# Second chunk's rows split between GpSimd and VectorE, and a reordered last finish, in a transformer layer kernel

## The reference, cut to what matters

```python
x = x + attn(layernorm(x), w_qkv, w_out)      # 16 heads of 8, rotary embedding, causal
h = layernorm(x)
logits = h @ router_W.T + router_b            # 6 experts
gate = softmax(logits); keep the 2 largest
w = kept / (sum(kept) + 1e-6)
low = (h @ routed_A[e].T) for each e          # rank 16
x = x + h @ base_W.T + base_b                 # base
      + (h @ shared_A.T) @ shared_B.T         # shared, rank 16
      + sum_e w[e] * (low[e] @ routed_B[e].T) # routed
```

## Time and profile before

| | us |
|---|---|
| median of 3 runs | 298.48 |
| lowest, highest | 298.29, 298.51 |
| profiled execution, device time | 298.24 |
| its span in the trace | 296.5 |

### The profile page before, as it was taken

How to read it: one execution, slowest core, us unless ns; L and a number is a source line. 1 busy time by engine, 2 the same in 40 slices (tenths; PEclk the granted TensorE clock), 3 DMA queues, 4 the chain that set the end, 5 groups by cost and what they waited for, 6 DMA issues and landing times.

```text
span 296.5 us, 7512 instructions
## 1 busy us (share of the span) xinstructions
PE 279.1 (94%) x3002; PEld 102.4 (35%) x3002; DVE 139.6 (47%) x420; ACT 267.3 (90%) x303; POOL 65.4 (22%) x145
## 2 busy tenths in 40 slices
PE   7869989899999999999999999999999999999996
PEld 2624332222132222122233124445433435445343
DVE  6876866687141558526171036522113262541054
ACT  8647899899999999999998999999999998999910
POOL 3576455514304012040030121010101010103000
PEclk9999999999999999999999999999999999999999
DMA  6443434004610000000000700001000001000000
GB/s 204 116 103 88 128 90 128 0 3 107 155 59 2 4 0 2 0 0 2 2 0 18 214 22 2 2 2 38 0 3 2 2 3 35 2 2 2 21 0 18
DMA packets 15256, 11.75 MB, mean 40 GB/s; under 512 B 2081, under 2 KB 14226, under 8 KB 15218
## 3 DMA queue, kind: packets, MB, share of 16 engines
q1 hardware_dynamic: 14594, 10.64, 13.0%
q0 software_dynamic: 192, 0.39, 0.5%
q10 hardware_dynamic: 432, 0.20, 0.3%
HBM read 3.88 MB, written 1.05 MB: 17 GB/s over the span
## 4 chain that ended last, share of the span: by engine, by line
PE 49%; ACT 25%; issue 14%; DVE 8%; DMA 2%; SPq 0%; ACTq 0%; DVEq 0%
ACT pbuf L713 24%; PE po L1147 22%; PE ps L1124 13%; PE ps L1270 2%; PE ps L1163 2%; PE pm L1163 1%; PE pm L1208 1%; PE pm L1157 1%; DMA qst<-parts 1%; PE pm L1169 1%; PE pm L1214 1%; PE pm L1222 1%; DVE rest L797 1%; DMA xs<-x_dram 1%; PE pm L1218 1%
## 5 line engine op out<-in xcount | busy, mean ns | idle before, releaser
L713 ACT ACTIVATE pbuf<-ps 128x1024 f32<-128x1024 f32 (+1 forms) x280 | 253.8, 1074 | 12.0 <-PE ps L1124 11.2
L1147 PE MATMUL po<-pbuf,va 128*9 128x256 f32 (+3 forms) x1792 | 143.8, 426 | 1.5 <-DVE oq L777 1.0
L1124 PE MATMUL ps<-qst,kst 64*128 64x256 bf16 (+3 forms) x896 | 97.6, 297 | 7.6 <-ACT pbuf L713 3.1
L649 POOL TENSOR_SCALAR_AFFINE_SELECT pbuf<-pbuf 128x256 f32<-128x256 f32 (+1 forms) x104 | 47.7, 481 | 196.4 <-ACT pbuf L713 195.2
L1124 PEld LDWEIGHTS ps<-qst,kst 64*128 64x128 bf16 x896 | 30.4, 94 | 106.3 <-ACT pbuf L713 80.5
L1147 PEld LDWEIGHTS po<-pbuf,va 128*9 128x9 f32 x1792 | 35.2, 89 | 55.9 <-issue 33.9
L777 DVE STREAM_TRANSPOSE oq<-po 128x256 f32<-128x256 f32 (+1 forms) x24 | 12.9, 538 | 65.4 <-PE po L1147 65.2
L1270 PE MATMUL ps<-kst 128*128 128x512 bf16 x46 | 11.3, 380 | 1.2 <-issue 1.2
L797 DVE TENSOR_TENSOR rest<-pm,sinT 32x512 f32<-32x512 f32 x16 | 11.0, 687 | 0.3
L1163 PE MATMUL ps<-xnT,wqkv 128*128 128x256 f32 (+1 forms) x24 | 8.3, 470 | 0.2 <-ACT xnT L683 0.2
L744 DVE BATCH_NORM_STATS2 stats<-xs 128x6 f32<-128x128 f32 x32 | 7.1, 281 | 2.4 <-DMA xs<-x_dram 1.3
(11 more groups left out here) (156 smaller groups left out, 186.3 us busy)
## 6 DMA issues: line engine op xcount, KB each, us to landing
qst<-parts SPq DMA_DIRECT2D x18, 128.0 KB, 2.8
kst<-parts SPq DMA_DIRECT2D x18, 128.0 KB, 2.6
xs<-x_dram SPq DMA_DIRECT2D x4, 256.0 KB, 3.3
cosT<-rope_c_dram SPq DMA_DIRECT2D x3, 256.0 KB, 4.0
sinT<-rope_s_dram SPq DMA_DIRECT2D x3, 256.0 KB, 4.5
out_dram<-xs SPq DMA_DIRECT2D x3, 256.0 KB, 2.3
kst<-parts SPq DMA_DIRECT2D x8, 64.0 KB, 2.2
qst<-parts SPq DMA_DIRECT2D x7, 64.0 KB, 2.5
```

What stands on the lines that cost most here:

```text
L649: ins = nc.gpsimd.affine_select(out=edge, in_=edge, compare_op=ALU.is_ge, fill=0.0, base=0, pattern=[[0, edge.shape[1]], [1, P]], channel_ ...
L713: nc.scalar.activation(probs[:, :, 0:width], ps[:, SLOT[u], :, 0:width], ACT.Exp, scale=SCALE).then_inc(exp_ready, 1)
L1124: ins = nc.tensor.matmul(ps[:, SLOT[u], e, place:place + n], side(kst, e)[:, g * 2 + pair, key:key + P], side(qst, e)[:, g * 2 + pair, q:q ...
L1147: ins = nc.tensor.matmul(po[32 * j:32 * j + DH + 1, q0:q0 + n], va[:, kt, g * GH + j, :], pbuf[:, u % NPB, at:at + n], start=blk["first"] ...
```

## The change

The inverse root of tiles 4 to 7 is a power on GpSimd. GpSimd normalises two of the four rows before its transfers, VectorE the other two after the first bound. TensorE turns them right behind the bound's sum, into `po`, and ScalarE copies them before unit 0. Q moves from unit 4 to unit 1, QS from 7 to 4. One bfloat16 filler at the flag becomes a float32 one, and the two after unit 0 are gone.

In the last finish the weights are reordered (routed, shared, logits). Logits are a product of their own; the 112 down columns come out turned, in one product; shared is added to base at once ("dense"). ScalarE scales dense, GpSimd adds the residual and the bias (a sixth small weight, `bbias`). VectorE spreads kept gates over 96 columns, TensorE turns these, VectorE multiplies them onto the turned down values, and the normaliser comes in with the scale of the last instruction. `WARM_U` is 5. The earlier finishes use the reordered weights and are otherwise as before.

```diff
-RD = R + E * R
+RT = E * R
+RD = RT + R
...
-WARM_O, WARM_X, WARM_R, WARM_U, WARM_F = 8, 7, 2, 14, 2
+WARM_O, WARM_X, WARM_R, WARM_U, WARM_F = 8, 7, 2, 5, 2
...
-WARM_FLAG = 4
+WARM_FLAG = 3
...
-WARM_UNITS = (2,)
+WARM_UNITS = ()
+ROWS_BY_POOL = 2
...
+HEAD_PRODUCTS = (("T", 2),)
...
-    (("T", 2), ("Q", 2), ("B", 1), ("QS", 2)),
+    (("Q", 2), ("B", 1), ("QS", 2)),
...
-    (2, 4, 4, 7),
+    (1, 4, 4),
...
-ACT_PLACES = (2, 9)
+ACT_PLACES = (9,)
...
-        def plain_third_order(engine, then, v, r, s, w):
-            then(engine.tensor_tensor(s, r, r, ALU.mult))
...
-        def inverse_sqrt(engine, then, at, nt):
-            v, r, s, w = var[:, at, 0:nt], rstd[:, at, 0:nt], sq[:, at, 0:nt], sq[:, 2, 0:nt]
-            then(engine.tensor_scalar(v, mv[:, at, 0:nt, 1], EPS, None, ALU.add))
-            then(engine.tensor_scalar(r.bitcast(I32), v.bitcast(I32), -0.5, float(0x5F3759DF), ALU.mult, ALU.add))
-            if engine is nc.gpsimd:
-                plain_third_order(engine, then, v, r, s, w)
-            else:
-                third_order(engine, then, v, r, s)
+        def inverse_sqrt(then, at, nt):
+            v, r, s = var[:, at, 0:nt], rstd[:, at, 0:nt], sq[:, at, 0:nt]
+            then(nc.vector.tensor_scalar(v, mv[:, at, 0:nt, 1], EPS, None, ALU.add))
+            then(nc.vector.tensor_scalar(r.bitcast(I32), v.bitcast(I32), -0.5, float(0x5F3759DF), ALU.mult, ALU.add))
+            third_order(nc.vector, then, v, r, s)
+        def inverse_sqrt_by_power(then, at, nt):
+            v = var[:, at, 0:nt]
+            then(nc.gpsimd.tensor_scalar(v, mv[:, at, 0:nt, 1], EPS, None, ALU.add))
+            then(nc.gpsimd.tensor_tensor(rstd[:, at, 0:nt], v, minus_half[:, 0:nt], ALU.pow))
...
+            if (name, c) == HEAD_PRODUCTS[0]:
+                return po[:, :]
...
-        def end_banks():
-            return ps[:, 1, 0, :], ps[:, 0, 0, :]
+        def dense_banks():
+            return ps[:, 0, 0, 0:P], ps[:, 1, 0, 0:P]
+        def gate_banks():
+            return pm[0:RT, 0:P], ps[0:RT, 0, 1, 0:P]
+        def routed_banks():
+            return ps[:, 2, 0, 0:P], ps[:, 2, 1, 0:P]
...
-            for dst, src in ((wout, w_out), (wdown, w_down), (wup, w_up), (wbase, w_base), (rbias, router_b)):
+            for dst, src in ((wout, w_out), (wdown, w_down), (wup, w_up), (wbase, w_base), (rbias, router_b),
+                             (bbias, base_b)):
...
+            then(nc.gpsimd.memset(minus_half[:, :], -0.5))
...
-            inverse_sqrt(nc.gpsimd, then, 1, TC)
+            inverse_sqrt_by_power(then, 1, TC)
+            for t in range(ROWS_BY_POOL):
+                normal_row(nc.gpsimd, xn[:, 1, t, :], 1, t, TC + t).then_inc(second_rows, 1)
...
-            for t in range(TC):
-                normal_row(nc.gpsimd, xn[:, 1, t, :], 1, t, TC + t).then_inc(second_rows, 1)
...
-            pool.wait_ge(end_scale, 1)
-            nc.gpsimd.tensor_tensor(low_rank[:, 0:END_TILES, RD], var[:, 0, 0:END_TILES], rstd[:, 0, 0:END_TILES],
-                                    ALU.mult).then_inc(end_deviation, 1)
+            for t in range(END_TILES):
+                pool.wait_ge(end_scaled, t + 1)
+                nc.gpsimd.tensor_tensor(ln[:, t, :], xs[:, END + t, :], ln[:, t, :], ALU.add).then_inc(end_summed_up, 1)
+            pool.wait_ge(ffn_in, 16 * 6)
+            for t in range(END_TILES):
+                pool.wait_ge(end_summed_up, t + 1)
+                nc.gpsimd.tensor_tensor(xs[:, END + t, :], ln[:, t, :], bbias[:, :], ALU.add).then_inc(end_biased, 1)
...
-                    nc.scalar.copy(xnT[:, chunk(p) % 2, :], pm[:, :]).then_inc(second_input, 1)
+                    nc.scalar.copy(xnT[:, chunk(p) % 2, :], product_bank(name, p)).then_inc(second_input, 1)
...
+            copy_product(*HEAD_PRODUCTS[0])
...
+            act.wait_ge(end_down, 1)
+            nc.scalar.copy(lowT[0:RD, 2:2 + END_TILES, :].rearrange("p t d -> p (t d)"),
+                           po[0:RD, 0:END_TILES * P]).then_inc(end_low, 1)
...
-            by_tile = pm[:, 0:END_TILES * P].rearrange("p (t d) -> p t d", t=END_TILES)
-            nc.scalar.copy(low_rank[:, 0:END_TILES, 0:R], by_tile[:, :, 0:R]).then_inc(end_shared, 1)
-            act.wait_ge(end_low_turned, 2)
-            nc.scalar.copy(lowT[0:RD + 1, 1, :], po[0:RD + 1, 0:P]).then_inc(end_low_last, 1)
+            act.wait_ge(end_scale, 1)
+            for t in range(END_TILES):
+                act.wait_ge(end_dense, t + 1)
+                nc.scalar.activation(ln[:, t, :], dense_banks()[t], ACT.Copy, scale=rstd[:, 0, t:t + 1]).then_inc(end_scaled, 1)
...
+            def step(ins):
+                steps[0] += 1
+                ins.then_inc(vec, 1)
+                return steps[0]
...
-                    routed = low_rank[:, 0:nt, R:RD].rearrange("p t (e r) -> p t e r", e=E)
+                    routed = low_rank[:, 0:nt, 0:RT].rearrange("p t (e r) -> p t e r", e=E)
...
-                dve.wait_ge(ffn_in, 16 * 5)
-                dve.wait_ge(end_down, 1)
+                dve.wait_ge(ffn_in, 16 * 6)
+                dve.wait_ge(end_raw, 1)
...
-                    ins = nc.vector.scalar_tensor_tensor(lg[:, t, :], by_tile[:, t, RD:RD + E], scale[:, t:t + 1],
+                    ins = nc.vector.scalar_tensor_tensor(lg[:, t, :], by_tile[:, t, 0:E], scale[:, t:t + 1],
...
-                then(nc.vector.tensor_reduce(top, mine, AX.X, ALU.max))
-                nc.vector.tensor_tensor(less, mine, top.unsqueeze(2).broadcast_to([P, nt, E]),
-                                        ALU.subtract).then_inc(end_logits, 1)
...
-                then(nc.vector.tensor_tensor(lead, other, this, ALU.subtract))
+                topped = step(nc.vector.tensor_reduce(top, mine, AX.X, ALU.max))
+                led = step(nc.vector.tensor_tensor(lead, other, this, ALU.subtract))
+                dve.wait_ge(vec, topped)
+                nc.vector.tensor_tensor(less, mine, top.unsqueeze(2).broadcast_to([P, nt, E]),
+                                        ALU.subtract).then_inc(end_logits, 1)
+                dve.wait_ge(vec, led)
...
+                for t in range(nt):
+                    nc.vector.scalar_tensor_tensor(low_rank[:, t, 0:RT].rearrange("p (e r) -> p e r", e=E),
+                                                   kept[:, t, :].unsqueeze(2).broadcast_to([P, E, R]), 1.5,
+                                                   share[:, t, :].unsqueeze(2).broadcast_to([P, E, R]),
+                                                   ALU.is_lt, ALU.mult).then_inc(end_kept, 1)
...
-                then(nc.vector.scalar_tensor_tensor(kept, kept, 1.5, share, ALU.is_lt, ALU.mult))
-                then(nc.vector.tensor_reduce(top, kept, AX.X, ALU.add))
-                then(nc.vector.scalar_tensor_tensor(total, total, 1e-6, top, ALU.mult, ALU.add))
-                then(nc.vector.reciprocal(total, total))
-                then(nc.vector.tensor_tensor(share, kept, total.unsqueeze(2).broadcast_to([P, nt, E]), ALU.mult))
-                dve.wait_ge(end_shared, 1)
-                nc.vector.tensor_tensor(low_rank[:, 0:nt, R:RD].rearrange("p t (e r) -> p t e r", e=E),
-                                        by_tile[:, :, R:RD].rearrange("p t (e r) -> p t e r", e=E),
-                                        gate[:, 0:nt, :].unsqueeze(3).broadcast_to([P, nt, E, R]),
-                                        ALU.mult).then_inc(end_routed, 1)
-                dve.wait_ge(end_low_turned, 1)
-                nc.vector.tensor_copy(lowT[0:RD + 1, 0, :], pm[0:RD + 1, 0:P]).then_inc(end_low, 1)
+                dve.wait_ge(end_kept, nt)
+                then(nc.vector.tensor_reduce(top, low_rank[:, 0:nt, 0:RT:R], AX.X, ALU.add))
+                normal = step(nc.vector.scalar_tensor_tensor(total, total, 1e-6, top, ALU.mult, ALU.add))
+                dve.wait_ge(end_low, 1)
...
+                    dve.wait_ge(end_gates, t + 1)
+                    nc.vector.tensor_tensor(lowT[0:RT, t, :], gate_banks()[t], lowT[0:RT, 2 + t, :],
+                                            ALU.mult).then_inc(end_gated, 1)
+                    if t == 0:
+                        dve.wait_ge(vec, normal)
+                        turned = step(nc.vector.reciprocal(total, total))
+                dve.wait_ge(vec, turned)
+                then(nc.vector.tensor_tensor(total, total, scale[:, 0:nt], ALU.mult))
+                for t in range(nt):
+                    dve.wait_ge(end_biased, t + 1)
...
-                    nc.vector.scalar_tensor_tensor(xs[:, END + t, :], last[t][:, 0:P], scale[:, t:t + 1], xs[:, END + t, :],
+                    nc.vector.scalar_tensor_tensor(xs[:, END + t, :], routed_banks()[t], total[:, t:t + 1], xs[:, END + t, :],
...
+            dve.wait_ge(second_rows, 1)
+            for t in range(ROWS_BY_POOL, TC):
+                normal_row(nc.vector, xn[:, 1, t, :], 1, t, TC + t).then_inc(second_rows, 1)
...
+                        pe.wait_ge(v_ready, 2)
...
```

(76 more changed lines are left out.)

6 lines of the change are left out of this document (3 added, 3 removed).

## The result

The changed kernel takes 297.21 us (median of 8, 297.02 to 297.56) against 298.34 (median of 8) of the kernel before in the same set: 1.13 us less, ratio 0.9962 with a 95% interval of 0.9953 to 0.9971. The span of its profiled execution is 295.5 us, 1.0 shorter.

What follows compares the result with a forecast made beforehand. TensorE and ScalarE were taken to share the bounding chain, with small instructions at the finish. Head -0.57 + 0.35 = -0.2 and finish -0.6 gave -0.8, taking the median 298.48 to 297.7; range 296.8 to 298.8.

Steps and rivals of the forecast that it cites:

- A: Whole kernel: head and finish both about as forecast, -0.6 to -1.1 us, 297.4 to 297.9; chance 0.40.
- B: Key addition and scale product both uncontended, d near 0: -0.57 - 0.9 = -1.5, 297.0; chance 0.20.
- Rival C: Finish, last tile's wait for `end_biased`: GpSimd's additions decide the end; 298.4 at p = 0.8, 299.2 at 0.93; chance 0.18.
- p: Finish: price of one GpSimd addition of 128 x 128, taken as 0.5 us, floor about 0.3, ceiling 0.93.
- the replay: Head, units 0 to 8 stepped through without d: unit 8 starts at 25.2 against 25.77, -0.57 us.
- half of QS: Head: QS (1.10 us) no longer stands between units 7 and 8; unit 8 gains 0.57, half of it.
- d: Head: lateness of unit 0's start, by filler queue (0.36) or last transfer (0.23); taken +0.35, range 0 to +0.65.
- Rival E: Head: VectorE's first key addition waits a whole GpSimd row, 0.8 instead of 0.28; sum -0.3, 298.2; chance 0.05.

Runs made afterwards that it cites:

- the last experiment: Changed kernel with two more unused, waited-for GpSimd additions of 128 x 128 per tile ahead of each bias addition: 298.55 us, ratio 1.0006.
- the run with the cheap root: Changed kernel with GpSimd's power replaced by a product of the same operands (inverse root wrong, only time of use): 296.87 us, ratio 0.9942.
- r1: The changed kernel itself run once more, in the second set, against the kernel before: 297.25 us, ratio 0.9963.
- e1: The kernel before with the head's edits alone and the old finish: 297.76 us, ratio 0.9973.

## Why the prediction was right or wrong

The time was forecast at 297.7 with 296.8 to 298.8 as its range, "faster" being likeliest; measured 297.21. The direction was right, and the gain was 1.13 instead of 0.8: the finish gave what was forecast, the head about 0.6 instead of 0.2. The result lies between rivals A (297.4 to 297.9) and B (297.0). Both of B's conditions came true, unit 0 about on time and the scale product not held up; its 0.9 for the finish did not.

**The finish: right, in part by luck.** Forecast -0.6, measured -0.55. The masks were over at 290.7, the transposes came behind the five fillers, as forecast. In the time of the profile of before (0.39 later at the logits) they started at 291.78 instead of the forecast 291.52: the dense products took 0.64 up to the first filler and not 0.55, and the fillers 1.08 up to the transposes and not 0.92. The last instructions started at 293.14 (forecast 293.1). Two errors cancel in that: the last product came 0.26 late as well, and the product of normaliser and scale was not held up (0.16). The addition was put at 0.5 by halving the variable part of the two-operation rows; it is 0.43 for one of two in a row and 0.45 for one alone. The estimate of 0.48 from the 2.6 cycles per element of the Trainium skill (GPSIMD Engine Reference, "Performance versus the Vector engine") was the nearer one. Rival C, which put the end on GpSimd from p = 0.62, has its mechanism shown by the last experiment and its condition not met.

**The head from unit 0 to unit 8: right in sum, wrong in its parts.** Forecast -0.57, measured -0.61, with unit 8 waiting for unit 6's exponential, as replayed. But the replay has unit 2's scores 1.76 behind unit 0 and its exponential 0.23 later than before; measured they stand 1.52 behind it (1.51 before) and the exponential follows without a gap, so that unit 5 comes about 0.2 earlier than before where the replay had no gain. Those 0.2 don't arrive at unit 8, since its scores start 0.28 after unit 6's exponential and not 0.05. Two errors cancel again. And the step "half of QS" was too simple: with QS back at unit 7 only 0.23 is lost, while T, the fillers and Q's new place free the same stretch. What the replay didn't hold at all is the clock, which fell in 11 of 24 executions with QS late and in none with QS at unit 4.

**d, the lateness of unit 0: the term that was mis-sized.** It was put at +0.35 from a contended addition (0.28), a float32 filler of 1.10 and a late last transfer (0.23, where its own landing at 18.72 instead of 18.44 gives 0.28). The power took 1.04 instead of 0.3, so the rows weren't beside the key addition but beside that of the queries, which lost 0.03 in after; had they been at the keys, the run with the cheap root shows that the addition need not lose anything. The filler takes 0.86. Like against like, unit 0 moves by -0.13 (after against before, both waiting for the transfer) and by +0.22 (r1 against the finish alone, both waiting for the queue), and within one head it moves more than that, up to 15.30 in e1. Total time leaves about zero: 1.06 of the 1.13 is accounted for without d. With d = 0 the sum of the prediction is 1.2.

**The lock.** The runs show that one engine waits for the other: the addition lost between nothing and 0.29, or the row beside it 0.24 to 0.30 (1.02 to 1.09 instead of 0.79), and only when they started close together. The small product of VectorE took 0.16 to 0.44 and in all twelve profiles with the new finish ended 0.02 behind the end of a GpSimd addition of 0.45. The Trainium skill (SBUF — State Buffer, "two separate sides") has a lock here that the first to start holds for the whole instruction. The small product agrees with it. The addition beside the rows doesn't: it never lost a row's 0.79, it ended inside the row that held it up, and in six profiles it was the row that paid although it had started first. Rival E, 0.8 for the addition, falls with that. What sets the length of the wait is open. The power's lower bound of 0.20 and upper of 3.3 held; below 2 us it was said to cost nothing, and GpSimd indeed still waits for the parts.

## What to carry to other kernels

When an engine's work is moved into an idle stretch, replay the waits of the other engine as well: of the 1.26 us (0.66 of T, 0.60 of fillers) taken off TensorE between units 0 and 8, 0.61 came out, and only with QS moved too; the rest went into waiting for ScalarE's two slots. Count fillers as work once the wait that they bridge gets shorter; here two too many cost 0.44 us by the profiles (0.56 between the medians), nearly as much as the whole new finish gained. Look at single executions with their clocks, not only at medians: the schedule that kept TensorE busy for 2.42 of 4 us was within 0.2 us of the other in 13 of 24 executions (median 297.36) and about 1.8 us slower in the rest (median 299.11). And a duration read beside another engine is one outcome: the same addition of one head took 0.72 in one profile and 0.44 in another.

## What was not expected of the hardware

A power of 4 elements per partition on GpSimd takes 1.04 us, five times a product of the same operands (0.20), and so is cheaper than the eleven steps (3.3 us) but not cheap. VectorE's addition of two SBUF operands beside a GpSimd row takes 0.42 to 0.72 for the same shape; when it is short, the row that starts beside it takes 1.02 to 1.09 instead of 0.79. And with QS late 11 of 24 executions of one program have a lower mean clock; in the one that was profiled TensorE fell to 1.2 GHz at the end of 4 us in which it was busy 60% of the time, and in the profile of another, as busy, it stayed at 2.4 GHz.
